# A decoder layer on one core: gates brought to tokens by 4-byte DMA elements, and a new order of shares, memory and scans

## Time and profile before

| | us |
|---|---|
| three runs | 1304.98 median, 1303.05 to 1307.32 |
| the profiled execution | 1301.37 |
| its span | 1299.6 |
| PE busy | 1269.3 (98%) |
| POOL, DVE, ACT busy | 754.7 (58%), 730.2 (56%), 460.3 (35%) |
| chain that ended last | PE 92%, DVE 3%, issue 2% |

### The profile page before, as it was taken

The page is one execution under the profiler, slowest core; times in us unless marked ns, Lnnn a source line. Parts: engine busy times, 40 slices in busy tenths (PEclk is TensorE's granted clock), DMA queues, the critical chain, the costliest instruction groups (busy, mean ns, idle before and its releaser), DMA issues.

```text
span 1299.6 us, 19475 instructions
## 1 busy us (share of the span) xinstructions
PE 1269.3 (98%) x6850; PEld 1032.9 (79%) x6850; DVE 730.2 (56%) x1269; ACT 460.3 (35%) x629; POOL 754.7 (58%) x519
## 2 busy tenths in 40 slices
PE   8889999999999999889999999999999999999998
PEld 7668888888888888768888888888788888888886
DVE  5688888888887888862343333343333423433324
ACT  5223332333333332443433434433434335344330
POOL 4766666667666666537537456274284376364551
PEclk9989999999999999989999999999999999999999
DMA  8666666666666664527207125135053071071210
GB/s 281 157 148 150 156 151 152 153 155 154 154 146 159 144 156 106 178 90 242 74 1 266 65 82 186 65 133 199 2 185 147 1 266 67 18 249 65 88 74 33
DMA packets 132612, 172.08 MB, mean 132 GB/s; under 512 B 13692, under 2 KB 75980, under 8 KB 132556
## 3 DMA queue, kind: packets, MB, share of 16 engines
q1 hardware_dynamic: 132556, 171.30, 45.8%
HBM read 137.44 MB, written 17.05 MB: 119 GB/s over the span
## 4 chain that ended last, share of the span: by engine, by line
PE 92%; DVE 3%; issue 2%; POOL 1%; DMA 1%; ACT 1%; SPq 0%; POOLq 0%; DVEq 0%
PE qk_ps L86 9%; PE qk_ps L88 9%; PE qk_ps L87 9%; PE v_ps L86 7%; PE v_ps L88 6%; PE v_ps L87 6%; PE gate_ps L86 5%; PE gate_ps L87 5%; PE gate_ps L88 5%; PE y_ps L86 3%; PE y_ps L87 3%; PE y_ps L88 3%; PE s_ps L86 3%; PE s_ps L88 3%; PE s_ps L87 3%; PE turn L1359 2%
## 5 line engine op out<-in xcount | busy, mean ns | idle before, releaser
L937 POOL TENSOR_TENSOR w_lo<-w_raw,w_hi 128x2048 fp32r<-128x2048 f32 x31 | 143.4, 4626 | 73.1 <-ACT w_hi L707 73.1
L929 POOL TENSOR_TENSOR w_lo<-w_raw,w_hi 128x2048 fp32r<-128x2048 f32 x32 | 148.0, 4625 | 15.8 <-ACT w_hi L717 15.8
L1015 DVE TENSOR_TENSOR_SCAN decays<-f_all,diag 128x384 f32<-128x384 f32 x128 | 150.3, 1214 | 0.6
L86 PE MATMUL qk_ps<-xT_parts,wqkv_hi 128*128 128x256 f32 x512 | 149.6, 292 | 0.9 <-DVE wqkv_lo L974 0.8
L1208 DVE CAST hid_hi<-gate_ps 128x512 fp32r<-128x512 f32 x62 | 42.9, 692 | 189.8 <-ACT gate_ps L741 189.6
L88 PE MATMUL qk_ps<-xT_parts,wqkv_lo 128*128 128x256 f32 x512 | 144.8, 283 | 0.0
L87 PE MATMUL qk_ps<-xT_parts,wqkv_hi 128*128 128x256 f32 x512 | 144.5, 282 | 0.0
L1208 DVE CAST hid_hi<-v_ps 128x512 fp32r<-128x512 f32 x62 | 42.9, 692 | 175.5 <-ACT v_ps L741 175.5
L901 POOL TENSOR_TENSOR rstd_b<-mean_var_b,ln_eps_b 128x4 f32<-128x4 f32 x15 | 3.7, 245 | 213.2 <-DVE mean_var_b L1193 213.2
L847 POOL TENSOR_TENSOR rot<-rot 128x256 f32<-128x256 f32 x64 | 70.3, 1099 | 95.9 <-DVE rot L1042 93.2
L741 ACT ACTIVATE gate_ps<-gate_ps,b_cols 128x512 f32<-128x512 f32 x64 | 42.2, 659 | 190.8 <-PE gate_ps L88 190.8
(11 more groups left out here) (228 smaller groups left out, 3175.4 us busy)
## 6 DMA issues: line engine op xcount, KB each, us to landing
w_raw<-in_w SPq DMA_DIRECT2D x64, 1024.0 KB, 7.5
f_all<-f_dram SPq DMA_DIRECT2D x16, 1024.0 KB, 4.8
qkT<-rot SPq DMA_DIRECT2D x256, 64.0 KB, 2.0
xT_raw<-in_xT SPq DMA_DIRECT2D x16, 512.0 KB
x_both<-in_x SPq DMA_DIRECT2D x16, 512.0 KB
f_all<-f_dram SPq DMA_DIRECT2D x16, 512.0 KB, 6.0
c_both<-in_ctx_in SPq DMA_DIRECT2D x16, 512.0 KB, 11.9
x_dram<-res SPq DMA_DIRECT2D x16, 512.0 KB, 12.5
```

The lines of the kernel that those rows point to most:

```text
L86: eng.matmul(out, lhs_hi, rhs_hi, start=first, stop=False)
L929: pool.tensor_tensor(w2_lo[s % 2][:], w2_raw[s % 2][:], w2_hi[s % 2][:].bitcast(F32), ALU.subtract)\
L937: pool.tensor_tensor(w1_lo[s % 2][:], w1_raw[s % 2][:], w1_hi[s % 2][:].bitcast(F32), ALU.subtract)\
L1015: dve.tensor_tensor_scan(decays[:, n, :], f_all[:, n, :], diag[:], 0.0, ALU.mult, ALU.add).then_inc(decay_done, 1)
```

## The change

Of steps 2 to 15, `turn_gates` goes. Instead `store_f` stores 16 rows (f and g), and a new `load_g` reads g back with tokens on partitions, in two DMAs of 1024 elements of 4 bytes. The shares of these steps come in another order: k, k, v, q, q, v in place of v, k, k, v, q, q. `cross_memory` comes ahead of `project_out` (steps 1 to 15), `gate_products` no longer waits for `token_gates` but for the sum of the gates, and DVE's order is written out anew for each kind of step. In steps 0 and 1 scans 2 and 3 come earlier, `out_weights_low` moves on POOL behind all eight scans of sequence 0, `context_low` behind two rotations, and SP holds back step 1's loads until f has landed. In the tail `weigh` comes ahead of norms, and POOL does `context_low(15)` ahead of `split_w2`.

```diff
-SHARES = ((2, 0), (1, 0), (1, 1), (2, 1), (0, 0), (0, 1))
+FIRST_SHARES = ((2, 0), (1, 0), (1, 1), (2, 1), (0, 0), (0, 1))
+SHARES = ((1, 0), (1, 1), (2, 0), (0, 0), (0, 1), (2, 1))
...
-                sp.dma_start(f_dram[b.odd].rearrange("(h t) -> h t", h=NH), gates[0:NH, :]).then_inc(f_stored, 16)
+                sp.dma_start(f_dram[b.odd].rearrange("(h t) -> h t", t=L), gates[0:2 * NH, :]).then_inc(f_stored, 16)
...
+            def load_g(b):
+
+                rows = f_dram[b.odd, NH * L:2 * NH * L].rearrange("(h t) -> t h", t=L)
+                for j in range(NT):
+                    sp.dma_start(g_raw[:, j, :], rows[j * P:(j + 1) * P, :], allow_slow_non_contiguous=True).then_inc(g_in, 16)
...
+                if b.n == 1:
+                    sp.wait_ge(f_in, 32 * 2)
                 if (b + 1).within(B):
                     store_rms(b + 1)
...
                     spread_f(b + 1)
+                    load_g(b + 1)
                     spread_o(b + 1)
...
                 if (b - 1).within(B):
                     grow_memory(b - 1)
                 if b.n == B - 1:
+                    square_ctx(b)
                     split_w2(Step(0), 0)
-                    square_ctx(b)
...
+                    if b.n == 1:
+                        pool.wait_ge(decay_done, NH)
+                        out_weights_low()
+                        residual(b)
                     if b.n >= 1:
                         x_low(b + 1)
                 if b.n == B:
-                    split_w2(Step(0), 0)
+                    pool.wait_ge(u_done, (b - 2).after(NT, NT))
+                    context_low(b - 1)
...
+                if b.n == 1:
+                    context_low(b - 1)
...
-                dve.wait_ge(gates_turned, b.after(1, 1))
+                if b.n <= 1:
+                    dve.wait_ge(gates_turned, b.after(1, 1))
+                else:
+                    dve.wait_ge(g_in, (b - 2).after(16 * NT, 16 * NT))
...
+            def second(b):
+                weigh_pair(b - 1, 0)
+                o_row(b)
+                scans(b - 1, 4, 5)
+                weigh_pair(b - 1, 1)
+                token_gates(b)
+                gate_v(b, 0)
+                scans(b - 1, 6, 7)
+                y_low(b - 1, 0)
+                rope_parts(b, 0)
+                rope_parts(b, 1)
+                weigh_pair(b - 1, 2)
+                clear_f(b)
+                scans(b, 0, 1)
+                y_low(b - 1, 1)
+                scans(b, 2, 3)
+                weigh_pair(b - 1, 3)
+                gate_v(b, 1)
+                y_low(b - 1, 2)
+                rope_parts(b, 2)
+                scans(b, 4)
+                y_low(b - 1, 3)
+                rope_parts(b, 3)
...
+            def middle(b, last):
+                add_memory(b - 2)
+                norm_stats(b - 2, 1)
+                weigh_pair(b - 1, 0)
+                weigh_pair(b - 1, 1)
+                rope_parts(b, 0)
+                y_low(b - 1, 0)
+                rope_parts(b, 1)
+                clear_f(b)
+                scans(b, 0, 1)
+                weigh_pair(b - 1, 2)
+                token_gates(b)
+                gate_v(b, 0)
+                if last:
+                    token_stats()
+                    token_means()
+                y_low(b - 1, 1)
+                scans(b, 2, 3)
+                if not last:
+                    scans(b, 4, 5)
+                weigh_pair(b - 1, 3)
+                rope_parts(b, 2)
+                y_low(b - 1, 2)
+                rope_parts(b, 3)
+                scans(b, 4 if last else 6)
...
+            def behind(b):
+                weigh_pair(b, 0)
+                norm_stats(b - 1, 0)
+                weigh_pair(b, 1)
+                add_memory(b - 1)
+                y_low(b, 0)
+                weigh_pair(b, 2)
...
-                    if n == 2 and b.n >= 1:
+                    if n == 2 and b.n == 1:
                         turn_gates(b)
...
                     gate_products(b + 1)
+                if (b - 1).within(B) and b.n != B:
+                    cross_memory(b - 1)
                 if (b - 1).within(B):
                     project_out(b - 1)
...
-                if (b - 1).within(B) and b.n != B:
-                    cross_memory(b - 1)
```

More of the change, by code:

```diff
@@ L666, in body @@
                         y_high(b - 1, c)
-                    if b.n == 1 and c == 0:
+                    if b.n == 1 and c == 1:
                         square_ctx(b - 1)
@@ L868, in body @@
                 if b.n == B:
[L869 removed]
+                    pool.wait_ge(u_done, (b - 2).after(NT, NT))
+                    context_low(b - 1)
                 if (b - 2).within(B):
                     norm_scale(b - 2)
[L872 to L874 removed]
+                if b.n == B:
+                    split_w2(Step(0), 0)
+                if 2 <= b.n <= B - 1:
                     context_low(b - 1)
@@ L890, in body @@
                     residual(b)
-                    out_weights_low()
                 if (b + 1).within(B) and b.n >= 1:
@@ L1152, in body, with weigh_pair, scans @@
+            def weigh_pair(b, c):
+                weigh(b, 2 * c)
+                weigh(b, 2 * c + 1)
+            def scans(b, *heads):
+                for n in heads:
+                    scan(b, n)
+            def body(b):
                 if b.n == -1:
@@ L1155, in body @@
                     weights_low(0)
-                if (b + 1).within(B):
                     sum_gates(b + 1)
-                if b.within(B) and b.n != 0:
-                    scan(b, NH - 1)
-                if b.n == B:
-                    split_hidden(Step(0), 1)
-                if (b - 1).within(B):
-                    for j in range(NT):
-                        add_residual(b - 1, j)
-                        if b.n == B - 1:
-                            token_low(Step(0), 2 * j)
-                            token_low(Step(0), 2 * j + 1)
-                    norm_stats(b - 1, 0)
+                elif b.n == 0:
+                    first(b)
+                elif b.n == 1:
+                    second(b)
+                elif b.n < B:
+                    middle(b, b.n == B - 1)
+                elif b.n == B:
+                    behind(b - 1)
+                else:
+                    add_memory(b - 2)
+                    norm_stats(b - 2, 1)
@@ new lines, in middle @@
+            def middle(b, last):
+                add_memory(b - 2)
+                norm_stats(b - 2, 1)
+                weigh_pair(b - 1, 0)
+                weigh_pair(b - 1, 1)
+                rope_parts(b, 0)
+                y_low(b - 1, 0)
+                rope_parts(b, 1)
+                clear_f(b)
+                scans(b, 0, 1)
+                weigh_pair(b - 1, 2)
+                token_gates(b)
+                gate_v(b, 0)
+                if last:
+                    token_stats()
+                    token_means()
+                y_low(b - 1, 1)
+                scans(b, 2, 3)
+                if not last:
+                    scans(b, 4, 5)
+                weigh_pair(b - 1, 3)
+                rope_parts(b, 2)
+                y_low(b - 1, 2)
+                rope_parts(b, 3)
+                scans(b, 4 if last else 6)
+                y_low(b - 1, 3)
+                if last:
+                    gate_v(b, 1)
+                    scans(b, 5, 6)
+                    add_residual(b - 1, 0)
+                    token_low(Step(0), 0)
+                    token_low(Step(0), 1)
+                    scans(b, 7)
+                    add_residual(b - 1, 1)
+                    token_low(Step(0), 2)
+                    token_low(Step(0), 3)
+                else:
+                    sum_gates(b + 1)
+                    gate_v(b, 1)
+                    scans(b, 7)
+                    add_residual(b - 1, 0)
+                    add_residual(b - 1, 1)
+                    norm_stats(b - 1, 0)
```

107 lines of the change are left out of this document (33 added, 74 removed).

## The result

The changed kernel takes 1288.16 us (median of 4 runs, 1287.34 to 1289.56) where the kernel before takes 1305.99 (4 runs, 1303.05 to 1307.32): a ratio of 0.9867, 95% interval 0.9849 to 0.9884. That is faster by 17.8 us or 1.3%. I had predicted 1300.5, in a range of 1289 to 1309. The profiled executions differ by less: 1288.53 against 1301.37, 12.8 us. Both numbers have to be explained, the 12.8 and the 5 on top.

The account below looks back on a forecast made before the run. PE was taken to bound the kernel, with DVE becoming the steady loop's other bound. Head +1.2, steady steps 0 and tail -5 made -3.8 us, taken off the 1304.98 median: 1301, rounded to 1300.5, range 1289 to 1309.

Parts of the forecast that it names:

- the reference: The profiled execution of the kernel before, 1301.37 us, against which the -3.8 was summed; 3.6 below the median of the runs.
- the tail: Steps 15 and 16: waits, half clock and turn gone, -12.65, new waits +6.65; with a possible clock dip, -5 us.
- The steady step: Steps 2 to 14: removed turn offset by new waits, sum 0.0 a step; 0 us over 13 periods, -3 to +4.
- the turn: PE's turning of v's gates (`turn_gates`), removed from 14 steps: 0.75 us less in each.
- two new waits: PE waiting for DVE in each steady step: 0.55 us at the second scores, 0.15 at the memory.
- The rival with no wait: No wait appears in the steady steps; PE saves 0.69 in each of 13, 9 us: 1292. Chance 0.17.
- The 4-byte reads: Reading g back, 2048 elements a step: 2.8 us taken, 62 us as high bound, hidden at no cost.
- the head: Up to the end of step 1's projection: 79.8 against 78.64 before, +1.2 us, -3 to +3.
- the new waits: Tail waits of PE: 0.55 and 1.2 in step 15; 1.9, 1.4 and 1.6 in step 16; 6.65 us in all.
- a dip of the clock: In the tail, one fall of PE's clock may come back, taking the gain from -6 to -5 us.
- The experts: The expert products behind the tail: not touched by the change, 0 us.
- head and tail give back more: Rival: POOL and DVE meet less in head and tail, 6 us more gain: 1295. Chance 0.13.

Follow-up runs that it names:

- Experiment 6: The changed kernel with v's token gates computed on ACT instead of DVE in steps 2 to 15: 1285.12 us.
- experiment 7: The changed kernel with DVE weighing the first two heads ahead of the norm statistics in steps 2 to 15, not behind them: 1280.70 us.
- experiment 8: The changed kernel with each 4-byte load issued twice, the second into a tile nobody reads, and the gates waiting for all four: 1288.61 us.
- experiment 9: The changed kernel with DVE's order around step 16 as in the kernel before, POOL's new order kept: 1288.23 us.
- experiment 1: The kernel before, unedited, profiled a second time: 1304.93 us over 10 runs; this profiled execution took 1306.80.
- experiment 2: The kernel before plus one wait: in step 1 POOL stands until scan 7 of sequence 0 is done: 1301.21 us beside 1305.77.
- experiment 3: The changed kernel with steps 2 to 14 as in the kernel before; step 15 keeps its turn of the gates too: 1293.00 us.
- experiment 4: The changed kernel with v's gates turned by PE in all steps again, without the 4-byte loads, other orders kept: 1299.15 us.

## Why the prediction was wrong

Two steps of the prediction failed: the reference, one profile's head carried over to the median (5 of the 17.8 us), and the tail, whose term was mis-sized (-9.1 measured, -5 forecast). Here is all of it term by term, in the profiled executions. I had -3.8 us and they show -12.8 (1288.53 - 1301.37).

**The steady step was right.** Predicted: -0.75 for the turn, two new waits of 0.55 and 0.15 at the second scores and at the memory, sum 0, period 32.8 to 33.4. Measured: period 32.98 or, from end of projection to end of projection (78.27 to 506.78), 32.96; both waits where they were put, 0.37 and 0.28 on average. Experiment 6 removes the second and gets 0.3 a step, experiment 7 removes both and gets 0.65. The rival with no wait was wrong; it is what experiment 7 made of it. 13 periods: -1.2 in place of 0.

**The 4-byte reads** were rightly put at no cost: hidden, with room for as many again. Their size was not right: each load lands 4.8 to 6.3 us after issue, and the two together take about 6.5 (79.96 to 86.48), where I took 2.8 for both. They are there between T + 8 and T + 11, within the T + 13 that I allowed. One cost I did not see: reading the gates from SBUF makes DVE's small operation wait for POOL (last section).

**The tail: the mis-sized term.** -9.1 where I had -5. Three causes. First, a mistake of account, 1.36 us: I measured the head up to the end of the projection, with a memory now ahead of it (+1.36 in the head), and started the tail from there, where the kernel before still has that memory to do; I never took it off. Second, the new waits were put in the right places, at the memory of step 15 (1.2, measured 1.09), at the start of step 16 behind w1's low part (1.9, measured 1.03, then 1.12 at the first expert product where I had 1.4 at the second scores) and at the fourth scores (1.6, measured 1.10), and with 0.55 against 0.19 ahead of them they sum to 4.5 in place of 6.65. Third, I took 1 us for a dip of the clock, and none came in this profile. That was luck: behind the same two waits the clock fell to 0.50 in three others (experiments 6, 8 and 9). The three make 4.5, and 4.1 was to be explained. These waits are the column's; by starts, as in the steady step, they are about 0.3, 1.3, 1.2, 1.2 and 1.2, 5.1 in all (an estimate, with the usual distances taken from steps without a wait), and the three causes then make 3.9.

**The head, and the reference, the step that failed most.** I predicted f at 53.6, PE going on at 64.0 and the memory at 70.6; they came at 54.0, 63.55 and 69.86. The end of the projection came at 78.27 in place of 79.8: half clock cost 1.6 in place of 2.3, and the rest is those 0.7. That is -0.4 against the first profile in place of +1.2. But what failed is the reference: the sum was made "against the profiled execution", and its -3.8 was taken off the median as it was. The one profile's head rested on scans 6 and 7 meeting POOL once; in the second profile they meet it twice, and the projection of step 1 starts 4.8 us later (experiment 1); one wait takes 4.6 us off the median (experiment 2). The profile was 3.6 us under the median of its kernel, I had noted this, and I should have asked which row could move. The changed kernel's scans 6 and 7 of sequence 0 meet no POOL operation: its profiled execution is 0.4 above its median. This is most of the 5 us between 12.8 and 17.8: by the estimate in experiment 2 some 4 of them; where the rest lies is open.

**The experts** gave 2.3 us that I had at 0, since the change does not touch them; 1.8 is a gap in PE's stream (last section), 0.5 was not followed.

So the rival "head and tail give back more" comes nearest, though with more than its 6 us and only partly by its cause: 13 of 17.8 us stay when the steady steps are put back (experiment 3).

## What to carry to other kernels

When an engine's slack is half a microsecond, taking time off the bottleneck moves the bound to the next chain, and the gain has to be bought there: two lines on DVE, worth 7.5 us on top of them, were worth more than the moves in the steady steps (4.8 by experiment 3). When a profile is several us under its kernel's median, look for the two instructions on different engines whose order within it could flip, before you carry a difference over to the median. And when a piece of work changes sides of the mark from which stretches are measured, count it in every stretch.

## What the runs showed of the hardware

*A small operation pays for where its input lies.* DVE's scaling of 128x8 gates by two scalars took 276 to 1407 ns (median 773) from SBUF in the changed kernel, and 270 to 286 ns from PSUM in experiment 4 (least/median/most, first and last start):

```profile
L1016 DVE TENSOR_SCALAR g_tok<-g_raw,rms x28: 276/773/1407, 95.0 to 522.5; 128x8 f32<-128x8 f32 x28
```

```profile
L1011 DVE TENSOR_SCALAR g_tok<-gate_ps,rms x32: 270/274/286, 25.5 to 531.2; 128x8 f32<-128x8 f32 x32
```

The change moved that input from one to the other. The Trainium skill, VectorE: DVE Perf Modes, section Why PSUM operands drop a tier, says that the mode which uses both SBUF read ports is closed to an operand in PSUM; and SBUF — State Buffer, section SBUF: two separate sides, that an operation in such a mode and a GpSimd operation exclude each other. By that rule the one from SBUF waits for POOL and the one from PSUM doesn't; the trace agrees. The second scaling of 260.23 runs from 260.58 to 261.36, beside a POOL operation from 260.58 to 261.33; in experiment 4 one from PSUM runs from 96.60 to 96.87 in the middle of a POOL operation from 96.26 to 96.99.

*Half a microsecond can flip 5.* Two scans that start at 47.58 take 3.92 us, and at 48.04 they take 5.76, beside the same POOL work; through a queue of DMAs behind them this became 4.8 us.

*A load with other transfers queued behind it landed late:* the second part of f took 11.3, 13.7 and 12.1 us with 4-byte stores and the loads of x and context queued behind it, 6.0 where SP held them back until f was there, in four profiles of the same load. Whether the stores or the loads did it was not separated.

*A gap without a releaser at one place.* PE stands for 1.5 to 1.9 us between two expert matmuls, at 937.3 in the first profile of before, with no engine or DMA named. It is in all five profiles of kernels that turn gates in each step (both of before, experiments 2, 3 and 4) and in none of the nine others. What it is stays open; nothing was tried on it.
